# A four-layer metaformer block on one core: a recurrent layer swept in other segments, and streaming matmuls added to an attention's waits

## The reference

```python
def _L0_ffn_ref(x, W, V, gamma, beta):
    Wx = jnp.einsum('bti,hi->bth', x, W)
    ...
    Wx = ((flat - mean) * jax.lax.rsqrt(var + BN_EPS) * gamma + beta).reshape(B, T, H)
    Vt = V.T
    def step(yt, wx_t):
        yt = jax.nn.sigmoid(wx_t + yt @ Vt)
        return (yt, yt)
    y0 = jnp.zeros((B, H), dtype=Wx.dtype)
    _, ys = jax.lax.scan(step, y0, jnp.swapaxes(Wx, 0, 1))
    return jnp.swapaxes(ys, 0, 1)
```

## Time and profile before

| | |
|---|---|
| time, median of 3 runs | 974.67 us (972.47 to 975.45) |
| the profiled execution | 975.6 us, its span 973.8 us |
| TensorE's mean granted clock | 0.974 of full speed |
| PE busy | 889.0 us (91%), 6191 matmuls |
| DVE busy | 414.4 us (43%) |
| ACT busy | 446.7 us (46%) |
| POOL busy | 239.2 us (25%) |

### The profile page before, as it was taken

The page is one execution under the profiler, slowest core; times in us unless marked ns, Lnnn a source line. Parts: engine busy times, 40 slices in busy tenths (PEclk is TensorE's granted clock), DMA queues, the critical chain, the costliest instruction groups (busy, mean ns, idle before and its releaser), DMA issues. The chain is left out here.

```text
span 973.8 us, 15415 instructions
## 1 busy us (share of the span) xinstructions
PE 889.0 (91%) x6191; PEld 518.6 (53%) x6272; DVE 414.4 (43%) x714; ACT 446.7 (46%) x1498; POOL 239.2 (25%) x144
## 2 busy tenths in 40 slices
PE   8778889888989888899999999999999999999887
PEld 5336667767845444344444444455555544554543
DVE  5699999999966753500000000002005400202763
ACT  5777777776636531333333333333333333334641
POOL 4149999998910000300000000000000000000410
PEclk9989999999999996999999999999999999999987
DMA  3110000000000000200000000000000000000000
GB/s 82 23 43 2 1 1 1 1 1 1 1 7 1 1 25 11 83 1 1 1 1 1 1 1 1 1 1 1 1 1 1 1 1 1 1 1 2 1 25 11
DMA packets 10220, 8.30 MB, mean 9 GB/s; under 512 B 7246, under 2 KB 8510, under 8 KB 10052
## 3 DMA queue, kind: packets, MB, share of 16 engines
q1 hardware_dynamic: 10148, 7.31, 3.1%
HBM read 5.47 MB, written 0.26 MB: 6 GB/s over the span
## 5 line engine op out<-in xcount | busy, mean ns | idle before, releaser
L908 PE MATMUL L2p_z<-stream 128*128 128x512 bf16 x880 | 342.2, 390 | 0.0
L950 ACT ACTIVATE L2yx<-L2p_z 32x2 f32<-32x2 f32 x1024 | 165.3, 161 | 323.0 <-PE L2p_z L927 323.0
L927 PEld LDWEIGHTS L2p_z<-L2yx,L2v 64*32 64x32 f32 x2048 | 137.6, 104 | 224.7 <-ACT L2yx L950 218.5
L927 PE MATMUL L2p_z<-L2yx,L2v 64*32 64x2 f32 x2048 | 225.5, 178 | 16.9 <-ACT L2yx L950 15.9
L788 POOL TENSOR_TENSOR hc<-hs,cb 128x1024 f32<-128x1024 f32 x64 | 149.6, 2363 | 4.4 <-DVE hs L729 4.4
L558 PEld LDWEIGHTS p_y<-ident,hc 128*128 128x128 f32 x1024 | 123.2, 192 | 16.5 <-POOL hc L788 9.1
L1641 DVE COPY xn_one<-L2yx 32x512 f32<-32x512 f32 (+1 forms) x2 | 0.8, 384 | 302.7 <-ACT L2yx L950 302.7
L558 PE MATMUL p_y<-ident,hc 128*128 128x128 f32 x1024 | 125.4, 276 | 4.3 <-POOL hc L788 4.3
L1641 POOL COPY xn_one<-L2yx 32x128 f32<-32x128 f32 x1 | 0.3, 284 | 484.2 <-SPq L1984 484.2
L729 DVE TENSOR_TENSOR_SCAN hs<-d_a,p_bb 128x1024 f32<-128x1024 f32 x48 | 109.8, 2287 | 6.2
L908 PEld LDWEIGHTS L2p_z<-stream 128*128 128x128 bf16 x943 | 90.1, 96 | 15.1
(11 more groups left out here) (522 smaller groups left out, 898.2 us busy)
## 6 DMA issues: line engine op xcount, KB each, us to landing
y_l<-in_pick SPq DMA_DIRECT2D x1, 768.0 KB
b_parts<-part SPq DMA_DIRECT2D x6, 128.0 KB, 2.3
c_parts<-part SPq DMA_DIRECT2D x6, 128.0 KB, 2.4
pos<-in_pos SPq DMA_DIRECT2D x1, 512.0 KB, 3.6
ao<-in_at_o SPq DMA_DIRECT2D x1, 512.0 KB, 4.0
L1w<-in_L_w SPq DMA_DIRECT2D x1, 297.0 KB
L3w<-in_L_w SPq DMA_DIRECT2D x1, 297.0 KB
above<-in_x SPq DMA_DIRECT2D x2, 128.0 KB, 3.1
```

The costliest lines, as they stand in the source:

```text
L908: pe.matmul(p_z[:, 1, 0:each], stream[:, 0:128], stream[:, 0:each], start=True, stop=True)
L927: pe.matmul(p_step[:, t % 2], v[:, 0:C], yx[:, NB * t:NB * (t + 1)], start=True, stop=True).then_inc(s("preact"), 1)
L950: act.activation(yx[0:C, NB * (t + 1):NB * (t + 2)], p_step[:, t % 2], ACT.Sigmoid).then_inc(s("state"), 1)
```

## The change

In the swept recurrence the segments are 8 tokens long in place of 16, so that there are 128 in place of 64; there are five sweeps in place of three, 40 steps in place of 48; and the streaming matmul of a step has 256 columns in place of 384. In the last attention streaming matmuls of 512 columns are added at six places of PE's order: 4 between `centre_new` and `sum_squares`, 2 in place of 1 behind it, 5 ahead of `mix_run(2)` (with a wait for DVE's last read of `atp_tok`), 2 behind `turn(23)`, 2 behind `values(23)` and 1 behind `turn_run(3)`.

```diff
--- before.py
+++ after.py
@@ -966,10 +966,10 @@
                     p_f = ps(tag + "p_f", [C, BANK], stack=s2)
                     p_g = ps(tag + "p_g", [R, BANK], stack=s2)
                     p_fill = ps(tag + "p_fill", [128, BANK], stack=s2)
-                    SEG = 16
+                    SEG = 8
                     NSEG = T // SEG
-                    SWEEPS = 3
-                    BESIDE = 384
+                    SWEEPS = 5
+                    BESIDE = 256
                     UNROLL = 16
                     guess = sb(tag + "guess", [C, NSEG - 1, NB], stack=s2)
                     differ = sb(tag + "differ", [C, NSEG - 1, NB], stack=s2)
@@ -2067,8 +2067,9 @@
                             last.then_inc(sig["at_mixed"], 1)
 
                         self.centre_new(pe)
+                        keep_streaming(pe, p_o, 4)
                         self.sum_squares(pe)
-                        keep_streaming(pe, p_o, 1)
+                        keep_streaming(pe, p_o, 2)
                         for s in range(6):
                             values(s)
                             keep_streaming(pe, p_q[:, 1], 2)
@@ -2116,13 +2117,18 @@
                         turn_run_back(2)
                         values(20)
                         values(21)
+                        pe.wait_ge(sig["at_max"], NJ * 12)
+                        keep_streaming(pe, self.p_tok[:], 5)
                         mix_run(2)
                         turn(22)
                         turn(23)
+                        keep_streaming(pe, self.p_tok[:], 2)
                         values(22)
                         values(23)
+                        keep_streaming(pe, self.p_tok[:], 2)
                         turn_across("x1", 1)
                         turn_run(3)
+                        keep_streaming(pe, self.p_tok[:], 1)
                         mix_across1(0)
                         turn_across("x3", 0)
                         turn_run_back(3)
```

## The result

The changed kernel took 1004.02 us (median of 4 runs, 1002.05 to 1004.80), the kernel before 975.06 beside it (4 runs, 972.47 to 977.26): a ratio of 1.030, 95% interval 1.028 to 1.032. Slower was forecast; 1004 lies 18 us above the forecast and 14 above its range. The profiled execution took 1003.75 us with a span of 1002.0; TensorE's mean granted clock was 0.946 in place of 0.974.

A forecast was written before the change was run, and what follows sets the result against it. The recurrence was taken as bound by the PE-ACT round trip, the attention by a chain through PE, ACT and DVE. 975.6 + 13.6 (sweeps, 10.5 of it stall and clock) - 2.7 (attention) = 986.5 profiled, 985.6 median; range 981.5 to 990.

The forecast's parts named there:

- the clock behind the stall: Sweeps behind the Gram matmul's wait: half clock for 4.6 us of work, 2.0 us lost, bounds 0 and 2.9.
- The step's width: Swept recurrence: a step with 128-column flocks takes 0.76 us in place of 0.605, about 1.3 at half clock.
- that rival: Rival for the swept recurrence: width is free, the step stays at 0.605 us, total 980.5; chance 0.05.
- A boundary between sweeps: Swept recurrence: each boundary waits for the second flock, +0.26 us, four times.
- The moved matmul: Gram matmul, now behind step 11, waits for DVE's copies, done at 315.7: a stall of 8.5 us.
- Wide steps without half clock: Swept recurrence: even without the stall and its clock, 40 wide steps end 2.9 us later than 48 narrow ones.
- no stall, wide step: Rival for the recurrence: DVE's products end before PE arrives, steps still wide; 975 us, no change; chance 0.03.
- The attention: Last attention: added streams hold the clock, queries 1.1 us earlier, tail 1.6 saved; -2.7 us taken, bounds -3.0 and +1.9.
- streaming gives nothing: Rival for the last attention: the clock falls all the same or streams stand in the way; 988.5 to 990; chance 0.08.
- The four streams ahead of `sum_squares` and the five ahead of `mix_run(2)`: Last attention: both sets hidden in PE's waits, four in 0.83 us for DVE, five taking 1.1 of 1.67 for ACT.
- The recurrence's states: Rival at the recurrence's comparison: states differ, so 1024 steps run one by one, +480 us; chance 0.02.

The follow-up runs named there:

- f1: Changed kernel with 34 streaming matmuls put ahead of the waiting Gram matmul, inside the stall: 986.88 us, 1.011 against the kernel before.
- f2: Changed kernel with 12 streaming matmuls put right behind the Gram matmul, stall kept: 988.77 us, 1.013 against the kernel before.
- e4: Changed kernel with 512 streaming columns in a step in place of 256, stall kept: 1007.58 us, 1.031 against the kernel before.
- e3: Changed kernel with the Gram matmul back behind step 27, 256 columns kept: 985.48 us, 1.009 against the kernel before.
- h1: Changed kernel with the Gram matmul behind step 23 and 384 streaming columns in a step: 979.57 us, 1.003 against the kernel before.
- e1: Changed kernel with the attention's added streams taken back, only the sweeps changed: 1003.75 us, 1.026 against the kernel before.
- e2: Kernel before with only the change's attention streams added, sweeps as before: 974.9 us, 0.998 against the kernel before.
- g2: Kernel before with only the streams of the attention's first part (4, and 2 in place of 1): 982.16 us median, 1.004 against the kernel before.
- f3: Kernel before with only the Gram matmul moved from behind step 27 to behind step 11: 1000.15 us, 1.022 against the kernel before.
- f4: Changed kernel with the Gram matmul behind step 21: 988.01 us, 1.013 against the kernel before.
- g1: Kernel before with only the ten streams of the attention's second half (5, 2, 2, 1): 976.85 us, 1.002 against the kernel before.
- i1: Kernel before with the change's attention streams and five more ahead of turn 16, over the middle wait: 972.13 us median, 0.9985 against the kernel before.

## Why the prediction was wrong

**The step that failed is the clock behind the stall.** The prediction took the earlier trace rows for it: "came back 4.6 us after work began", 2.0 us lost, at most 2.9. The clock was down from 306.3 to 360.9. The 28 steps took 36.9 us (316.51 to 353.45) where that step of the sum had 24.3; the compare and the streams behind them took 8.18 to the next block, where before's take 5.47 (326.98 to 332.45). That is +12.6 and +2.7 (0.25 of the latter was forecast). Added up for the profiled executions (1003.75 against 986.5, 17.2 us): 12.6 in the steps, 2.5 behind them, 0.5 because the steps behind the Gram matmul begin at 316.51 and not 316.05, 2.1 for the attention (below), less 0.5 in the other stages. f1 prices the lost clock by itself: 17.2 us. With the clock held the kernel takes 986.9, 1.3 above the forecast, and its recurrence is 11.0 over before's, where the forecast without its 2.0 for the clock had 11.6.

The row misled because of what ran when the clock came back, and the row says it: 17 streaming matmuls of 128x512 on the full array. The sweep's step is another kind of work, fp32 matmuls of 64 rows and 32 columns of weights with one stream between. f2 shows the two side by side behind the same stall. At half clock PE had no idle time left in a step (37.19 of 37.30), so more streaming per step had no room either (e4). I had bounded the cost with half as long again as that row, and no bound asked whether the clock would come back at all.

The Trainium skill, "TensorE: Matmul & The Clock Gate", section "What's actually happening", ties the clock to how busy TensorE has lately been and sets busy beside the full clock. The window of 37.30 us in this case differs: PE is busy in it by the records, and the clock is at 0.50. Which part of the work counts is not told by these runs; only that pure streaming did and these steps didn't.

The other steps:

- The step's width: 0.76 forecast, 0.76 measured, in after, e3 and f1. 1.3 at half clock: 1.29 to 1.32. The width is not free; that rival is out. PE is closer to being the bound than its forecast 0.70: with 384 columns it sets the step at 0.81 (h1), and with 256 it needs some 0.75, an estimate from h1 and e4. A boundary between sweeps cost 0.20 and not 0.26 (303.67 to 304.63 is 0.96). By the isolated gap in the Trainium skill, "TensorE: Matmul & The Clock Gate", section "Back-to-back issue gap", the step would have been 0.71 (an estimate); the rows of the same shapes were the better guide.
- The moved matmul: DVE ready at 315.7 forecast, 316.11 measured. PE's idle time was 7.42 and not 8.5 because its last two steps ahead of the stall ran at half clock; in e1 and f2, whose clock held so far, it was 8.42. That the clock falls was right; that it could fall ahead of the stall was not foreseen.
- Wide steps without half clock cost 2.4 us more than the narrow ones (f1); 2.9 forecast (its own terms, 13.6 less 10.5, give 3.1). The rival "no stall, wide step" would have been 975; e3 and h1 come nearest, at 985.5 and 979.6, each with something of its own late or longer.
- The attention: -1.1 forecast and -1.25 measured in the first part, -1.6 and -2.1 in the tail. The clock's fall in the middle (+2.8 after, +5.5 in e2 and g2) was in no term, so the part came to -0.6 and not to -2.7. The rival "streaming gives nothing" is what e2 measures, though not by its mechanism: each set gives somewhat more than was forecast where it stands, and half clock in the middle takes more than that back.
- The four streams ahead of `sum_squares` and the five ahead of `mix_run(2)` were hidden, as forecast: `sum_squares` begins 1.53 us into the attention before and after, and the middle takes 24.77 with the five (e4, f2) and without them.
- The recurrence's states did not differ: no step-by-step pass ran, which would have cost some 480 us.

## What to carry to other kernels

When a wait is uncovered on TensorE, price what runs behind it at half clock up to work that the trace shows to bring the clock back; don't carry over the time from a stretch of other work. If the wait can't be avoided, stream through it (f1, 17.2 us gained here), or right behind it (f2, 12.7 in the recurrence). An index written as a function of another constant (`2 * SEG - 4`) moves with it: check against the trace that what it waits for is still ready, and measure a streaming matmul by the stage after it as well as by its own.

## What the runs showed of the hardware

- TensorE stayed at half clock for 45 us behind the stall (316.2 to 360.9), the first 37 of them almost without idle time, and for 43 us behind that of f3, whose matmuls are narrow; 4.3 us of pure streaming brought it back, 3.3 us after it began (f2).
- A wait of 0.58 us in a loop of 0.76 us steps with 256 streaming columns was followed by 31 us at half clock (f4), and in the changed kernel's profile the clock fell in that loop ahead of any long wait; in e3 the same loop held the full clock for 34 us.
- The same wait of 1.26 us in the attention is followed by half clock in seven of the nine profiles with the first part's streams (e2, g2 and after among them) and in none of the four without (before, e1, f3, g1), though the work close around it is the same. Only where it is streamed over (i1) was a cause tested, in one profile. Why e4 and f2 hold the clock stays open.
